# Layer 0 attention: TensorE's steps taken in twos

## The reference, cut to what matters

```python
# query = _layernorm(x) (8, 256, 128), key = value = ctx_768 (8, 512, 96), 16 heads of 8
Qp = query @ Wq + bq
K  = _l2norm(key @ Wk + bk)            # over all 128 columns
V  = value @ Wv + bv
Q  = _l2norm(Qp)                       # over all 128 columns
scores = einsum('bhqd,bhkd->bhqk', Q, K) * 8 ** -0.5
out = einsum('bhqk,bhkd->bhqd', softmax(scores), V) @ Wo + bo
y   = layernorm(out + Qp) * ln_gamma + ln_beta
x   = x + y
```

## Time and profile before

| | us |
|---|---|
| median of 3 runs | 1791.3 (1790.86 to 1795.83) |
| the profiled execution | 1800.71 |
| span of its trace | 1798.7, mean granted TensorE clock 0.899 |
| PE busy | 1493.7 (83%) |
| PEld busy | 1036.9 (58%) |
| DVE busy | 1001.9 (56%) |
| ACT busy | 926.3 (51%) |
| POOL busy | 636.8 (35%) |
| layer 0 attention, first scores to last update of x | 48.8 to 261.6 |

### The profile page before, as it was taken

How to read it: one execution, slowest core, us unless ns; L and a number is a source line. 1 busy time by engine, 2 the same in 40 slices (tenths; PEclk the granted TensorE clock), 3 DMA queues, 4 the chain that set the end, 5 groups by cost and what they waited for, 6 DMA issues and landing times. The chain is left out here.

```text
span 1798.7 us, 30587 instructions
## 1 busy us (share of the span) xinstructions
PE 1493.7 (83%) x9887; PEld 1036.9 (58%) x9887; DVE 1001.9 (56%) x2428; ACT 926.3 (51%) x1912; POOL 636.8 (35%) x648
## 2 busy tenths in 40 slices
PE   2999974897258736699999988969999999999985
PEld 2444434796125425466777645546777777777764
DVE  2566536335566654466666634536666666666651
ACT  1677750432456463356665532326565666666642
POOL 3344413000000004156555512215564564554541
PEclk8799985898569957799999998979999999999997
DMA  4200000000000004000000000000000000000002
GB/s 134 68 1 0 1 1 1 1 0 24 0 0 1 0 0 115 24 1 1 0 0 0 1 1 1 0 1 1 1 1 0 0 0 0 0 0 0 1 1 71
DMA packets 29226, 20.30 MB, mean 11 GB/s; under 512 B 9205, under 2 KB 26206, under 8 KB 29150
## 3 DMA queue, kind: packets, MB, share of 16 engines
q1 hardware_dynamic: 29150, 19.34, 3.8%
HBM read 18.29 MB, written 1.05 MB: 11 GB/s over the span
## 5 line engine op out<-in xcount | busy, mean ns | idle before, releaser
L1397 POOL TENSOR_TENSOR l3a_prob<-l3a_prob,l3a_rinv 128x512 f32<-128x512 f32 x256 | 260.8, 1041 | 205.1 <-DVE l3a_rinv L1615 200.3
L1550 ACT ACTIVATE l3a_prob<-l3a_scores_ps,l3a_nmax 128x512 f32<-128x512 f32 x256 | 173.5, 684 | 140.8 <-DVE l3a_nmax L1609 140.8
L1609 DVE TENSOR_REDUCE l3a_nmax<-l3a_scores_ps 128x2 f32<-128x1024 f32 x128 | 150.9, 1220 | 84.2 <-PE l3a_scores_ps L1442 84.2
L843 ACT ACTIVATE l0a_prob<-l0a_scores_ps,l0a_k_scale 128x1024 f32<-128x1024 f32 x128 | 141.7, 1115 | 56.2 <-PE l0a_scores_ps L749 55.9
L1397 POOL TENSOR_TENSOR l2a_prob<-l2a_prob,l2a_rinv 128x512 f32<-128x512 f32 x128 | 130.2, 1042 | 92.6 <-DVE l2a_rinv L1615 91.9
L1453 PE MATMUL l3a_turned_ps<-const,l3a_prob 128*128 128x128 f32 x1024 | 156.2, 275 | 3.0 <-DVE l3a_probT L1621 0.9
L1453 PEld LDWEIGHTS l3a_turned_ps<-const,l3a_prob 128*128 128x128 f32 x1024 | 117.9, 140 | 26.9 <-DVE l3a_probT L1621 12.0
L1550 ACT ACTIVATE l2a_prob<-l2a_scores_ps,l2a_nmax 128x512 f32<-128x512 f32 x128 | 86.8, 685 | 76.1 <-DVE l2a_nmax L1609 76.1
L1464 PE MATMUL l3a_work_ps<-l3a_probT,l3a_v 128*64 128x256 f32 x1024 | 124.6, 385 | 1.6 <-ACT l3a_probT L1557 0.9
L1621 DVE COPY l3a_probT<-l3a_turned_ps 128x512 f32<-128x512 f32 x128 | 87.9, 687 | 51.9 <-PE l3a_turned_ps L1453 51.8
L1464 PEld LDWEIGHTS l3a_work_ps<-l3a_probT,l3a_v 128*64 128x64 f32 x1024 | 68.2, 136 | 51.9 <-issue 23.6
(11 more groups left out here) (604 smaller groups left out, 3681.6 us busy)
## 6 DMA issues: line engine op xcount, KB each, us to landing
l1f_w<-in_L_ffn_w SPq DMA_DIRECT2D x16, 256.0 KB, 2.9
l3f_experts_w<-in_L_ffn_W SPq DMA_DIRECT2D x32, 64.0 KB, 1.8
load_ctx_rows<-in_ctx SPq DMA_DIRECT2D x1, 1536.0 KB, 7.8
w_l_w<-in_L_ffn_W SPq DMA_DIRECT2D x1, 1024.0 KB
out_x<-x_tokens SPq DMA_DIRECT2D x1, 1024.0 KB, 4.5
const<-in_constants SPq DMA_DIRECT2D x1, 589.0 KB
w_l_wo<-in_L_xattn_Wo SPq DMA_DIRECT2D x1, 512.0 KB
l1a_raw_f<-in_L_xattn_W_f SPq DMA_DIRECT2D x1, 512.0 KB, 4.1
```

The costliest lines, as they stand in the source:

```text
L843: e.activation(prob[n % 4][:, :], sc[n % 2][:, :], ACT.Exp, scale=kscale[:, n % KT:n % KT + 1]).then_inc(m.prob_ready, 1)
L1397: e.tensor_tensor(prob[n][:, :], prob[n][:, :], bcast(rinv[:, n:n + 1], [P, S]), ALU.mult).then_inc(m.prob_ready, 1)
L1550: e.activation(prob[at][:, :], bank(u), ACT.Exp, bias=nmax[:, at:at + 1], accum_out=rsum[:, at:at + 1]).then_inc(m.exp_ready, 1)
L1609: e.tensor_reduce(nmax[:, at:at + 2], sps[:, i * 1024:(i + 1) * 1024].rearrange("p (h k) -> p h k", h=2), AX.X, ALU.max, negate=True).then ...
```

## The change

TensorE's list alone changes. A turn now takes two steps at a time, `n` and `n + 1` for odd `n`: the scores of `n + 1` and `n + 2`, the weighted sums of `n - 1` and `n`, the item of `n` and the item of `n + 1`. The projection of the next keys, the item of step 0, becomes the last item of the turn before (`between(b, STEPS)` does it for batch b + 2). Ahead of the first turn stand `scores(0, 1)` and `keys(10, 1)`, and behind the last one no `weighted` is left over. The number of instructions, their operands, and the lists of all other engines stay as they are.

```diff
+            def between(b, n):
+                before, after, after_that = parts(b)
+                if n == STEPS:
+                    if after_that:
+                        keys(0, b + 2)
+                    return
...
             def turn(b):
-                before, after, _ = parts(b)
-                last_item[:] = [("k_turned", b, 3), ("q_turned", b, 1)]
-                for n in range(STEPS):
-                    if n + 1 < STEPS:
-                        scores(b, n + 1)
-                    elif after:
-                        scores(b + 1, 0)
-                    if n > 0 or before:
-                        weighted(b, n - 1)
...
-                    if after and n == 0:
-                        keys(n, b + 1)
...
+                _, after, _ = parts(b)
+                last_item[:] = [("k", b + 1, 0) if after else ("k_turned", b, 3), ("q_turned", b, 1)]
+                for n in range(1, STEPS, 2):
+                    for k in (n + 1, n + 2):
+                        if k < STEPS:
+                            scores(b, k)
+                        elif after:
+                            scores(b + 1, k - STEPS)
+                    weighted(b, n - 1)
+                    weighted(b, n)
+                    between(b, n)
+                    between(b, n + 1)
...
             scores(0, 0)
+            scores(0, 1)
+            keys(10, 1)
             turns(e, turn)
-            weighted(B, -1)
             turn_pv(1, B - 1, 3)
```

More of the change, by code:

```diff
@@ L766, in weighted @@
                 last.then_inc(m.pv_ready, 1)
-            def turn(b):
-                before, after, _ = parts(b)
-                last_item[:] = [("k_turned", b, 3), ("q_turned", b, 1)]
-                for n in range(STEPS):
-                    if n + 1 < STEPS:
-                        scores(b, n + 1)
-                    elif after:
-                        scores(b + 1, 0)
-                    if n > 0 or before:
-                        weighted(b, n - 1)
[L778 to L785, removed]
-                    if after and n == 0:
-                        keys(n, b + 1)
[L788 to L797, removed]
@@ new lines, in between @@
+            def between(b, n):
[4 more added lines that the diff above has]
+                    return
+                if before and n == 1:
+                    turn_pv(n, b - 1, 3)
+                if before and n == 3:
+                    turn_o(n, b - 1)
+                if before and n == 4:
+                    output(n, b - 1)
+                if n in (6, 9, 13):
+                    turn_pv(n, b, (6, 9, 13).index(n))
+                if after and n == 2:
+                    values(n, b + 1)
+                if after and n == 5:
+                    tokens(n, b + 1)
+                if after and n == 7:
+                    queries(n, b + 1)
+                if after and n in (8, 10, 11, 14):
+                    turn_keys(n, b + 1, (8, 10, 11, 14).index(n))
+                if after and n in (12, 15):
+                    turn_queries(n, b + 1, (12, 15).index(n))
```

## The result

The changed kernel takes 1800.12 us (median of 6 runs, 1798.97 to 1803.37), the kernel before 1794.89 in as many (1790.86 to 1796.3): a ratio of 1.0035, 95% interval 1.002 to 1.005. So the change costs 0.35%. Forecast were 1790.7 and no change, with 1783 to 1799 as the range. Of the distance of 9.4 us, 3.6 are the base: the three runs of before that stood first lay low (1791.3). The other 5.8 are the change: in the main the term of the six periods, which had the wrong sign, and the term of the clock, which was too small.

The account below looks back on a forecast made before the run. The prediction took a loop through VectorE, GpSimd and TensorE as the bound of layer 0's attention. Savings of 1.8 + 1.3 + 0.5 = 3.6 us less 3.0 for the clock gave 1790.7 us from 1791.3, range 1783 to 1799.

Parts of the forecast that it names:

- the term of the six periods: Layer 0's attention: six periods between the seven turn_queries(.., 0), each 0.3 us shorter, 1.8 us saved.
- the term of the clock: After TensorE's wait before turn_queries: drops to 1.2 GHz in more batches, 3.0 us given back.
- The loop and its two arcs: Layer 0's attention: turn_pv(.., 3) to turn_queries, 17.70 us, and back to turn_pv, 7.85, set the period, 25.55.
- the first arc: From turn_pv(.., 3) to turn_queries: VectorE and GpSimd in turns, 17.70 us; TensorE's gains there become waiting.
- The sizes of the joins: TensorE's pairs: two scores 0.66 us, saving 0.20; two weighted sums 1.00, saving 0.14; two items save 0.15.
- the first batch: Clock low, TensorE itself the bound: three score pairs plus the sums' joins save 1.3 us, bounds 0 and 2.5.
- GpSimd's and VectorE's rows unchanged in length and order: Expected sign in the timeline after: both engines' instructions keep their durations and sequence.
- The second arc: From turn_queries to the next turn_pv(.., 3): TensorE's own work, 7.54 us against 7.85, 0.31 less.
- the second scores' wait for its exponential: In a pair, the second scores waits for the second exponential of the pair before: 0 to 0.1 us.
- 4 falls in six batches: Stretches at 1.2 GHz after TensorE's wait before turn_queries: 4 of 6 batches instead of 2, at 1.5 us each.
- Rival 2: Low clock after TensorE's wait before turn_queries in each of six batches, costing 6 to 15 us; 1794 to 1803; chance 0.20.

Follow-up runs that it names:

- second pair of profiles: The kernel before and the changed kernel run again unchanged on one chip: 1795.81 us and 1799.28 us (ratio 1.0027).
- single: Kernel before, order of single steps, with GpSimd's copy behind VectorE's split, turn_pv(.., 3) earlier, and VectorE's keys' copy in its wait for the norm's root: 1796.31 us, ratio 0.9992.
- late copy: Changed kernel with GpSimd's copy of the low value heads (L570) waiting until VectorE has split the queries: 1794.09 us, ratio to the kernel before 0.9989.
- after (twice): The changed kernel, profiled in two executions: 1800.12 us, ratio 1.0035, then 1799.28 us, ratio 1.0027.
- early turning: Changed kernel with turn_pv(.., 3) moved between the scores and the weighted sums of its pair: 1793.37 us, ratio to the kernel before 0.9984.
- half filled: Changed kernel with five extra matmuls, results unused, before turn_queries(12): 1797.98 us, ratio to the kernel before 1.0004.
- into the gap: Changed kernel with GpSimd's copy behind VectorE's split, turn_pv(.., 3) earlier, and VectorE's keys' copy in its wait for the norm's root: 1791.90 us, ratio 0.9971.
- before (twice): The unchanged kernel before, profiled in two executions: 1794.89 us, then 1795.81 us.
- filled: Changed kernel with ten extra matmuls, results unused, before turn_queries(12): 1797.03 us, ratio to the kernel before 1.0002.
- filling behind: Changed kernel with ten extra matmuls before turn_queries(12) and four more right behind it: 1803.72 us, ratio to the kernel before 1.0028.
- all three: Changed kernel with GpSimd's copy behind VectorE's split, turn_pv(.., 3) earlier, and eight extra matmuls before turn_queries(12): 1792.08 us, ratio to the kernel before 0.9976.
- before early: Kernel before with turn_pv(.., 3) moved ahead of the scores of step 1: 1793.21 us, ratio 0.9988.
- before filled: Kernel before with four extra matmuls, results unused, before its turn_queries(12): 1797.76 us, ratio 1.0011.

## Why the prediction was wrong

**What held.** The loop and its two arcs: filling the first arc cost nothing, filling the second its length, moving `turn_pv` shortened the period in both kernels. The sizes of the joins too: pairs of 0.66 and 1.00. TensorE's gain went in the main where it was said to go, into waiting.

**Right by luck: the first batch.** Up to `turn_queries` 2.4 us were saved (24.32 to 21.90 from the first scores; 1.3 forecast, bound 2.5), and 2.0 in the second pair of profiles. The forecast took this from the joins, with TensorE as the bound. The windows from the first scores to `turn_queries` of the kernel before again, of the changed one again, and of "single" (columns as in rows 8) say otherwise:

```profile
48.80:72.00 23.20, 23.20 (x163) 11.07 (x162) 11.06 (x29) 15.60 (x16) 7.68 (x8) 0.74 0.40 106
48.20:69.50 21.30, 19.42 (x164) 10.70 (x162) 10.56 (x29) 15.48 (x16) 8.56 (x9) 0.84 0.46 124
48.00:68.90 20.90, 20.90 (x163) 10.01 (x162) 11.44 (x29) 15.27 (x16) 7.71 (x8) 0.84 0.45 122
```

"Single" has TensorE's steps one at a time, as in the kernel before, and never waits there (20.90 busy of 20.90). At the same mean clock of 0.84 it is no slower than the pairs, which wait for 1.9 us. So the 2 us came with an earlier rise of the clock, and not from the joins. The clock rose 5.0 to 8.2 us after the first scores in all nine profiles with pairs, and 6.8, 12.1, 14.7, 18.2 and 18.3 us in the five without; that the pairs bring it on is likely, and not shown.

**The step that failed first: "17.6 to 17.7 from turn_pv(.., 3) to turn_queries", with "GpSimd's and VectorE's rows unchanged in length and order".** I took the first arc as fixed, because its lists were untouched and TensorE's inputs to it came early enough. An input that comes too early was not considered. The copy L570 on GpSimd had been kept back by TensorE alone, and released it ran into VectorE's scalings: +0.56, less the 0.13 to 0.15 that the earlier variance gave; the arc is 18.13. The late copy shows it: 17.58 with that one wait added. Times six periods that is 2.6 us. The kernel before's trace shows the price, and the prediction doesn't weigh it: in the prologue, at 41.4 us, the same two scalings take 1.76 us beside two instructions of GpSimd, and in each batch the variance takes 0.74.

The Trainium skill, page "SBUF — State Buffer", section "SBUF: two separate sides", says that VectorE in a two-port mode and GpSimd share a pair of ports by an exclusive lock, held for a whole instruction, and that the other one blocks fully. The rows agree: the first scaling, 0.29 us when alone, ends at about 200.3, just after the copy's end at 200.21, and the second is as short as ever. In which mode the scalings run, no run here shows.

**The second arc, forecast 7.54,** is 7.70. The term that was off is the second scores' wait for its exponential, put at 0 to 0.1: that pair takes 0.81 (179.29 to 180.10) instead of 0.66. This alone would have been within the bounds: with the late copy the period is 25.29. That it was forecast as 25.27 is in part luck, for the arcs are 7.71 and 17.58 and not 7.54 and 17.7: 0.15 too much was promised for the second, and 0.1 in the first, which the forecast mentions, wasn't counted.

**The clock was forecast in the right way and too low:** 4 falls in six batches against 2; measured 5 in both profiles, and in the two of before 2 and 1. At 1.3 us each here (27.1 - 25.84) and 1.5 before, it is 3.5 to 5 us and not 3.0. The prediction also miscounted the waits of 1.0 in the kernel before: there are five, and the sixth, at 228.8 us, is 0.34. The falls, with each kernel's longest wait of TensorE between 95 and 225 us:

| kernel | longest wait, us | falls in its profile |
|---|---|---|
| after (twice) | 2.7 | 5, 5 |
| late copy | 2.2 | 4 |
| early turning | 1.8 | 3 |
| half filled | 1.5 | 0 |
| into the gap | 1.2 | 0 |
| before (twice) | 1.1 | 2, 1 |
| filled, filling behind, all three | 0.8 | 0, 0, 0 |
| before early, single, before filled | 0.6 or less | 0, 0, 0 |

Idle time doesn't order them. Between 70 and 240 us "into the gap" has TensorE busy for 146.44 of 170 us and no fall, the second profile of before 164.59 and one. The longest wait orders them only from 1.8 us on: half filled and "into the gap" have longer waits than the kernel before, and no fall. What else decides isn't shown.

Together, by the second pair of profiles: 2.0 saved in the first batch, 6.9 lost over six periods (154.1 to 161.0), 0.8 saved at the end, 4.1 lost in the stage; by the first pair 1.6 lost (before had its two falls there). Timed it is 5.2 and 3.5. Rival 2 of the prediction named part of the mechanism, the low clock after the wait. Its price for the falls, 6 to 15 us, was too high; that the difference of 5 us lies in its range is owed to the periods, which it took as shorter. The collision, which also lengthened the wait from 2.2 to 2.7, wasn't among the cases.

**What stays open.** The text behind this stage is the same in all kernels, and yet it took from 1533.8 to 1538.5 us in the profiles, and the kernel before ran from 1790 to 1805 us. The four profiled executions don't show the difference of the medians at all (spans of 1798.7 and 1796.0 before, 1796.8 and 1796.3 after): what the stage loses there is made up behind it. That this is where the clock rises and falls in later stages is likely, and wasn't followed. So a difference of 2 us between two of these kernels isn't told apart by their medians; the periods in the profiles are. Of the 5.8 us that the forecast of the change was off, the stage shows 2.2 in the first pair of profiles and 4.7 in the second; the rest is open.

## What to carry to other kernels

Before shortening the busiest engine's groups, follow its one recurring wait back until it meets that engine again: only the part of its list between the wait's end and the loop's own item counts, and moving that item one place up was worth twice the joins here (0.6 to 0.7 a batch against 0.27). Of every instruction on the other engines that waits for the engine made faster, ask what it will run beside when it comes early. Fill a wait no further than it reaches: eight matmuls too many by 0.35 us cost that in every batch. Bunched work can make the same idle time into one long wait, and in these runs waits of 1.8 us and more cost TensorE its clock in most batches.

## What the runs showed that I had not expected

Useless matmuls made the kernel faster: ten before `turn_queries`, 2.46 us a batch, brought the ratio to the kernel before from 1.0027 to 1.0035 down to 1.0002, by keeping the granted clock at 1.00 from 70 to 240 us. And a GpSimd instruction of 0.82 us, started 0.06 us ahead of a VectorE scaling of 0.29, made that last 0.85. The same was seen at three other places, with other operands: the scalings of the norm, 1.36 for 0.60, the split of the queries, 1.20 for 0.69, and a variance of 2 columns, 0.74, which took 0.17 where GpSimd was at rest ("into the gap").
